# Weights of a linear layer summed over their bits and transposed on TensorE, in the first three tiles of an attention kernel

## What is computed

```
x = x + xattn(layernorm(x), ctx, ctx)                  # x, ctx: 4 x 1024 x 1024 fp32; 16 heads of 64, causal
soft   = sigmoid(pweight) - sigmoid(nweight)           # 1024 x 1024 x 4 bits, fp32
weight = einsum('oin,n->oi', soft, exps * sigmoid(mask_weight)) * scale
bias   = bit_ste(einsum('on,n->o', pbias - nbias, bexps)) * biasscale
x = x + layernorm(x) @ weight.T + bias
```

## Time and profile before

| | |
|---|---|
| median of 3 runs | 1310.44 us (1309.8 to 1312.69) |
| profiled execution | 1313.67 us, its span 1310.7 us |
| busy share of the span | PE 87%, DVE 82%, ACT 71%, POOL 46% |
| granted TensorE clock, mean | 0.944 of 2.4 GHz |
| chain that ended last | PE 62%, DVE 19%, issue 6%, ACT 5%, POOL 3%, DMA 3% |

### The profile page before, as it was taken

One profiled execution on the slowest core, in us unless ns is written; L12 is line 12 of the kernel. 1 busy time (PEld: TensorE's weight loads), 2 busy tenths in 40 slices (PEclk: granted clock), 3 DMA queues, 4 the chain that ended last, 5 costly groups with the idle time before them and its releaser, 6 DMA issues.

```text
span 1310.7 us, 28652 instructions
## 1 busy us (share of the span) xinstructions
PE 1144.8 (87%) x11088; PEld 848.5 (65%) x11088; DVE 1072.6 (82%) x1613; ACT 926.6 (71%) x2011; POOL 599.9 (46%) x717
## 2 busy tenths in 40 slices
PE   1555665589998999999999999999999999999998
PEld 1433444466766677777777677787776677777753
DVE  3588998878897688888898898888988888888861
ACT  1677787567776577777777777777787777777740
POOL 2378666533324574433324954433237744332241
PEclk9867767689999999999999999999999999999999
DMA  6899899243333675433324856434226854320113
GB/s 187 224 223 255 225 267 240 66 106 89 66 81 69 158 168 123 114 81 93 72 82 82 201 121 130 97 82 94 70 64 147 178 116 111 81 66 2 33 41 89
DMA packets 245622, 157.08 MB, mean 120 GB/s; under 512 B 220912, under 2 KB 220912, under 8 KB 245488
## 3 DMA queue, kind: packets, MB, share of 16 engines
q1 hardware_dynamic: 245488, 155.26, 49.5%
HBM read 67.15 MB, written 16.78 MB: 64 GB/s over the span
## 4 chain that ended last, share of the span: by engine, by line
PE 62%; DVE 19%; issue 6%; ACT 5%; POOL 3%; DMA 3%; SPq 1%; ACTq 0%; DVEq 0%; POOLq 0%
PE ffnb L433 20%; PE ptb L401 14%; PE oacc L415 7%; PE slot L388 7%; PE slot L389 7%; DVE pt_lo L570 5%; PE oacc L417 4%; DVE stats L584 3%; DVE mx L563 3%; ACT pt_hi L476 2%; PE slot L433 2%; PE slot L392 2%; DMA qt<-q 1%; DVE y L610 1%; DVE ring L619 1%
## 5 line engine op out<-in xcount | busy, mean ns | idle before, releaser
L570 DVE SCALAR_TENSOR_TENSOR pt_lo<-ptb,pt_hi 128x384 f16<-128x384 f32 (+2 forms) x688 | 382.9, 597 | 117.6 <-ACT pt_hi L476 115.4
L466 ACT ACTIVATE p<-slot,mx 128x512 f32<-128x512 f32 (+7 forms) x512 | 378.0, 747 | 96.1 <-DVE mx L563 94.1
L476 ACT ACTIVATE pt_hi<-ptb 128x384 f16<-128x384 f32 (+2 forms) x688 | 326.4, 527 | 150.2 <-PE ptb L401 149.4
L401 PE MATMUL ptb<-id,p 128*128 128x128 f32 x2304 | 340.8, 289 | 75.9 <-DVE pt_lo L570 75.0
L563 DVE TENSOR_REDUCE mx<-slot 128x1 f32<-128x640 f32 (+7 forms) x352 | 359.5, 1021 | 32.8 <-PE slot L392 30.2
L433 PE MATMUL ffnb<-wt,yt 128*128 128x512 f16 x1440 | 365.3, 381 | 18.6 <-DVE ring L619 15.6
L401 PEld LDWEIGHTS ptb<-id,p 128*128 128x128 f32 x2304 | 259.5, 146 | 87.6 <-issue 84.4
L388 PE MATMUL slot<-kt,qt 128*128 128x128 f16 (+3 forms) x1056 | 278.5, 293 | 38.8 <-DMA qs<-qt 26.5
L753 POOL TENSOR_TENSOR att<-osb 128x256 f32<-128x256 f32 x128 | 98.8, 772 | 398.9 <-ACT osb L483 375.8
L389 PE MATMUL slot<-kt,qs 128*128 128x128 f16 (+3 forms) x1056 | 278.4, 293 | 0.0
L415 PE MATMUL oacc<-v,pt_hi 128*128 128x128 f16 x2304 | 252.3, 224 | 15.3 <-ACT osb L483 13.4
(11 more groups left out here) (64 smaller groups left out, 976.8 us busy)
## 6 DMA issues: line engine op xcount, KB each, us to landing
ring<-in_x_dram SPq DMA_DIRECT2D x32, 512.0 KB, 4.9
cin<-in_ctx_dram SPq DMA_DIRECT2D x32, 512.0 KB, 4.2
qs<-qt SPq DMA_DIRECT2D x64, 256.0 KB, 3.8
out_dram<-ring SPq DMA_DIRECT2D x32, 512.0 KB, 2.9
v<-in_L_ffn_pweight_dram SPq DMA_DIRECT2D x16, 512.0 KB, 4.7
kt<-in_L_ffn_nweight_dram SPq DMA_DIRECT2D x16, 512.0 KB, 5.6
v<-in_L_ffn_nweight_dram SPq DMA_DIRECT2D x8, 512.0 KB, 7.6
kt<-in_L_ffn_pweight_dram SPq DMA_DIRECT2D x8, 512.0 KB, 4.5
```

Of the source, the lines that this page charges most:

```text
L401: last = pe.transpose(ptb[:, c % 2, at * P:(at + 1) * P], p32[:, j.par, k * P:(k + 1) * P], id32[:, :])
L466: last = nc.scalar.activation(p32[:, j.par, hh * j.keys:(hh + 1) * j.keys], slot[:, j.par, base:base + j.keys], ACT.Exp, bias=mx[:, j.par, ...
L476: nc.scalar.activation(pt_hi[:, j.par, P * blocks.start:P * blocks.stop], ptb[:, c % 2, 0:P * len(blocks)], ACT.Copy, scale=P_SCALE).then_ ...
L570: nc.vector.scalar_tensor_tensor(pt_lo[:, j.par, cols], ptb[:, c % 2, 0:P * len(blocks)], P_SCALE, pt_hi[:, j.par, cols], ALU.mult, ALU.su ...
```

## The change

- Chunks are taken in pairs, called units. Unit u goes with job u, for jobs 0 to 15, that is in tiles 0 to 2. There are 6 pairs of buffers.
- The product, the sum over bits and the DMA transpose of the weights are gone. In their place PE does 16 fp32 matmuls a unit: the stationary operand is the difference at one bit (128 weights with a step of 4 elements), the moving operand is the identity times that bit's coefficient, and the four bits add up in the PSUM bank `ffnb`. The result comes out transposed.
- ACT and DVE split it from PSUM straight into `wt` (512 elements a unit).
- `linear_plan` gives each tile from 4 on one linear layer: tile 4 gets one, tile 8 keeps one.
- SP loads x and context of tile 0 first, and the bias is made behind the first scores, in other banks.

```diff
-PAIRS = 4
+UNITS = CHUNKS // 2
+PAIRS = 6
...
 def linear_plan(t):
-    n = steps(t) if t < TILES else 0
-    if t < 5:
+    return [(t - 4, 0, steps(t))] if 4 <= t < TILES else []
...
-        pairs = [(as_f32(v16, 8), as_f32(v16, 9)), (as_f32(v16, 7), as_f32(kt16, 8)),
-                 (as_f32(kt16, 7), as_f32(kt16, 6)), (as_f32(yt, 0), as_f32(yt, 1))]
-        w32 = ring[:, 7, :]
+        pairs = [(as_f32(v16, 9), as_f32(v16, 8)), (as_f32(v16, 7), as_f32(kt16, 8)),
+                 (as_f32(kt16, 7), as_f32(kt16, 6)), (as_f32(v16, 6), as_f32(kt16, 5)),
+                 (ring[:, 7, :], ring[:, 6, :]), (as_f32(v16, 5), as_f32(yt, 0))]
+        coef_diag = as_f32(yt, 1)[:, 0:NBITS * P].rearrange("p (n q) -> p n q", n=NBITS)
         ones32 = y16[:, 0, 0:2, :].bitcast(F32).rearrange("p a b -> p (a b)")
         bits = y16[:, 1, 0, :].bitcast(F32).rearrange("p (a n) -> p a n", a=2)
-        bdiag = norm32[:, :].rearrange("p (j q) -> p j q", j=8)
+        bdiag = bias_row[:, :].rearrange("p (j q) -> p j q", j=8)
         coef = small[:, 14:18]
...
             def load_w(w):
-                reached(sp, w_sum, w - PAIRS + 1)
+                reached(sp, w_turned, (w - PAIRS) // 2 + 1)
                 sp.dma_start(pairs[w % PAIRS][0], pw_t[w // NWCH, w % NWCH]).then_inc(w_in[w % PAIRS], 16)
...
+            load_x(0)
+            load_c(0)
...
+            load_w(0)
             load_x(1)
-            load_w(0)
-            load_x(2)
-            load_w(1)
             turn_k(0)
             load_c(1)
+            load_w(1)
             turn_q(0)
             swap_q(0)
-            load_w(2)
             turn_k(1)
             load_c(2)
             turn_q(1)
+            load_w(2)
             load_w(3)
+            load_x(2)
+            load_w(4)
+            load_w(5)
...
+                    u = FIRST[t] + s + 3
+                    if u < UNITS:
+                        load_w(2 * u)
+                        load_w(2 * u + 1)
...
+            def weights(u):
+                if u == 0:
+                    pe.wait_ge(coef_step, NBITS)
+                    pe.wait_ge(bias_out, 2)
+                reached(pe, w_lo, u)
+                pe.wait_ge(d_ready, 2 * u + 2)
+                for b in range(4):
+                    a = pairs[(2 * u + b // 2) % PAIRS][0].rearrange("p (k n) -> p k n", n=NBITS)
+                    for n in range(NBITS):
+                        last = pe.matmul(ffnb[:, b * P:(b + 1) * P], a[:, b % 2 * P:(b % 2 + 1) * P, n],
+                                         coef_diag[:, n, :], start=n == 0, stop=n == NBITS - 1)
+                last.then_inc(w_turned, 1)
...
             pe.wait_ge(pool_const, 9)
+            scores(JOBS[0])
+            scores(JOBS[1])
             pe.wait_ge(bias_step, 18)
             for j in range(8):
-                last = pe.matmul(slot[:, 0, j * P:(j + 1) * P], ones32[:, :], bdiag[:, j, :], start=True, stop=True)
+                bank = oacc[:, j, :] if j < 4 else ffnb[:, (j - 4) * P:(j - 3) * P]
+                last = pe.matmul(bank, ones32[:, :], bdiag[:, j, :], start=True, stop=True)
             last.then_inc(bias_summed, 1)
...
+                if j.n < UNITS:
+                    weights(j.n)
...
-            def weights_high(o):
-                act.wait_ge(w_sum, NWCH * (o + 1))
-                reached(act, wt_in, 16 * o)
-                nc.scalar.copy(y16[:, 0, :, :], w32.rearrange("p (k c) -> p k c", c=P)).then_inc(w_hi, 1)
+            def weights_high(u):
+                act.wait_ge(w_turned, u + 1)
+                nc.scalar.copy(wt[:, 0, u % 2 * 4:u % 2 * 4 + 4, u // 2 * P:(u // 2 + 1) * P],
+                               ffnb.rearrange("p (k c) -> p k c", c=P)).then_inc(w_hi, 1)
...
+            c_split(0)
             act.wait_ge(small_in, 16 * 7)
             nc.scalar.activation(coef, small[:, 8:12], ACT.Tanh, scale=0.5).then_inc(coef_tanh, 1)
+            q_split(0)
+            chunk_tanh(0)
+            c_split(1)
+            q_split(1)
+            chunk_tanh(1)
+            exponentials(JOBS[0])
+            exponentials(JOBS[1])
             act.wait_ge(bias_summed, 1)
             nc.scalar.copy(bias_row[:, :].rearrange("p (q j) -> p j q", j=8)[:, 0:4, :],
-                           slot[:, 0, 0:512].rearrange("p (j q) -> p j q", j=4)).then_inc(bias_out, 1)
-            c_split(0)
-            q_split(0)
-            c_split(1)
-            q_split(1)
-            exponentials(JOBS[0])
-            exponentials(JOBS[1])
+                           oacc[:, :, :]).then_inc(bias_out, 1)
...
+                if 0 <= j.n - 1 < UNITS:
+                    weights_high(j.n - 1)
                 high_parts(j)
+                if j.n + 1 < UNITS:
+                    chunk_tanh(2 * j.n + 2)
                 if j.n + 2 < len(JOBS):
                     exponentials(JOBS[j.n + 2])
-                w = weight_step(t, s)
-                if w is not None:
-                    weights(w)
+                if j.n + 1 < UNITS:
+                    chunk_tanh(2 * j.n + 3)
...
-            def weights_sum(w):
-                a = pairs[w % PAIRS][0].rearrange("p (k n) -> p k n", n=NBITS)
-                dve.wait_ge(d_ready, w + 1)
-                nc.vector.tensor_tensor(a, a, coef.unsqueeze(1).to_broadcast([P, WCH, NBITS]), ALU.mult
-                                        ).then_inc(w_mul, 1)
-                reached(dve, w_lo, w // NWCH)
-                dve.wait_ge(w_mul, w + 1)
-                nc.vector.tensor_reduce(w32[:, w % NWCH * WCH:(w % NWCH + 1) * WCH], a, AX_X, ALU.add
-                                        ).then_inc(w_sum, 1)
-
-            def weights_low(o):
-                dve.wait_ge(w_hi, o + 1)
-                nc.vector.tensor_tensor(y16[:, 1, :, :], w32.rearrange("p (k c) -> p k c", c=P), y16[:, 0, :, :],
-                                        ALU.subtract).then_inc(w_lo, 1)
-
-            def weights(w):
-                if w >= 5 and w % NWCH == 1:
-                    weights_low((w - 5) // NWCH)
-                if 1 <= w <= CHUNKS:
-                    weights_sum(w - 1)
+            def weights_low(u):
+                dve.wait_ge(w_hi, u + 1)
+                rows, cols = slice(u % 2 * 4, u % 2 * 4 + 4), slice(u // 2 * P, (u // 2 + 1) * P)
+                nc.vector.tensor_tensor(wt[:, 1, rows, cols], ffnb.rearrange("p (k c) -> p k c", c=P),
+                                        wt[:, 0, rows, cols], ALU.subtract).then_inc(w_lo, 1)
...
+            dve.wait_ge(pool_const, 9)
+            for n in range(NBITS):
+                nc.vector.tensor_scalar(coef_diag[:, n, :], id32[:, :], coef[:, n:n + 1], None, ALU.mult
+                                        ).then_inc(coef_step, 1)
+            q_split(0)
...
+                if j.n + 1 < UNITS:
+                    difference(2 * j.n + 2)
                 if j.n > 1 and JOBS[j.n - 2].closes_group:
                     add_attention(JOBS[j.n - 2].group)
+                if j.n + 1 < UNITS:
+                    difference(2 * j.n + 3)
```

More of the change, by code:

```diff
@@ L119 @@
 BIAS = {4: 2, 8: 4, 16: 9}
-Y_LATE = {0: (10, 12, 14), 4: (12, 13, 14), TILES - 3: (12, 13, 14)}
+Y_LATE = {TILES - 3: (12, 13, 14)}
 def q_at(t, s, part):
[L127 to L130, removed]
+    return t + 2 < TILES and s == Q_STEPS[steps(t)][part]
 def y_begun(t, s):
@@ L241, in build @@
         bias_added, ffn_done, res_done = sem("bias_added"), sem("ffn_done"), sem("res_done")
-        th_ready, d_ready, w_mul, w_sum, w_hi, w_lo = (
-            sem("w_" + n) for n in ("tanh", "diff", "mul", "sum", "hi", "lo"))
+        th_ready, d_ready, w_turned, w_hi, w_lo = (sem("w_" + n) for n in ("tanh", "diff", "turned", "hi", "lo"))
         pool_const, coef_tanh, coef_step, bias_step = (
@@ L331, in _ @@
                     if s == 0:
-                        if t >= 6:
-                            for k, _, _ in linear_plan(t - 1)[-1:]:
-                                store(k)
+                        if t >= 5:
+                            store(t - 5)
                         if t + 1 < TILES:
                             swap_q(t + 1)
-                        if t == 8:
-                            turn_y(4)
-                    if s == (0 if 4 < t < 9 else n // 2):
-                        ahead = {5: 7, 6: 8, 7: 9, 8: 10}.get(t, t + 3)
-                        if t != 4 and ahead < TILES:
-                            load_x(ahead)
-                    if t == 8 and s == 3:
-                        store(3)
-                        load_x(11)
-                    w = weight_step(t, s)
-                    if w is not None:
-                        if w >= 1 and w + 3 < CHUNKS:
-                            load_w(w + 3)
-                        if w >= 5 and w % NWCH == 1:
-                            turn_w((w - 5) // NWCH)
+                    if s == n // 2 and t + 3 < TILES:
+                        load_x(t + 3)
                     if s == C_LO[n] and t + 3 < TILES:
@@ L669, in _ @@
```

(27 more changed lines are left out.)

65 lines of the change are left out of this document (17 added, 48 removed).

## The result

| | before | changed |
|---|---|---|
| median | 1310.59 us | 1300.01 us (1298.93 to 1301.84) |
| ratio | 1 | 0.9918 (0.9901 to 0.9935) |
| span of the profiled execution | 1310.7 us | 1298.0 us |
| first maxima of tile 0 / tile 4 / tile 10 | 36.0 / 185.6 / 460.0 us | 31.0 / 229.1 / 446.5 us |
| PE busy, granted clock | 87%, 0.944 | 94%, 0.991 |

The account below looks back on a forecast made before the run. DVE, carrying the weights, was taken to bound the stage before 263 us, PE the rest. 36 + 15 x 9.1 + 22.8 + 218.8 put tile 10 at 414.1, 45.9 us earlier: 1310.4 - 45.9 = 1264.5 us, range 1247 to 1303.

Parts of the forecast that it names:

- transfers that bind: Second rival, jobs with units: DMA transfers bound the period, 11 us a job, 1292 us (10.2 us, 1281); chance 0.20.
- Added on PE: PE's new unit matmuls in the first stage: 16 a unit, 59 to 118 us of PE in all.
- The first rival: Units on PE: strided fp32 loads don't hide, 1427 us, middle 1355; with PE always at 1.2 GHz (1325), chance 0.12.
- P: Period of a job with a unit, tiles 0 to 2: forecast 9.1 us, range 8.4 to 10.1 at chance 0.56.
- end of the first unit: Start of the kernel: unit 0 ends at 36 us, after tile 0's first maxima at about 23.5.
- rest of tile 3 to tile 4: After unit 15: six more jobs of tile 3 at 3.6 us plus 1.2 us of PE, 22.8 us.
- tiles 4 to 9: After the weights: one linear layer each, taking the 218.8 us of tiles 20 to 25.
- chain of tanh and differences: Unit's loop through PE, ACT and POOL at full clock: 17.5 us for two jobs, mean 8.1 us a job.
- the bank loop: At 1.2 GHz, unit j waits for the previous unit's low split from the single bank `ffnb`: 13.2 us a job.
- One job in five at 1.2 GHz: PE's clock in jobs with units: 0.8 x 8.1 + 0.2 x 13.2 = 9.1 us a job.
- the fourth rival: At tile 4: weights ready sooner, but late first y or low PE clock gives it back, no gain; chance 0.02.
- Break-even at P = 12.2: Jobs with units: a period of 12.2 us leaves tile 10 at 460 us, so no gain.

Follow-up runs that it names:

- the first experiment: Changed kernel with each unit matmul reading 128 contiguous elements as stationary operand instead of a step of 16 bytes (sums of other elements): 1270.2 us, ratio 0.9676.
- The bank-first run: Changed kernel with ACT copying the unit out before the attention group and DVE taking the low split before the maxima, same work: 1284.4 us, ratio 0.9784.
- the short units: For 290 to 327 GB/s: changed kernel with ACT's and DVE's unit work put first and one of four bits summed: 1258.4 us, ratio 0.9577.

## Why the prediction was right in its sign and wrong in its size

The direction and the stage were right, and the time lay in the range, which is luck: the upper end, 1303, had been set for transfers that bind, and it was PE that held the period at 10.9 us. The step that failed is the price under "Added on PE": "A unit has 16 matmuls: 7.4 us at 1.2 GHz, 3.7 us at 2.4 GHz". Measured are 7.7 us at either clock. The reading of the bias matmuls as 1.2 GHz ones was sound (a contiguous pass is 0.112 us at full clock and 0.213 at half in the first experiment, and theirs are 0.22 apart). What failed was to carry that price to an operand with a step of 16 bytes. The first rival named this mechanism, priced its far ends and gave it 0.12 on the slower side only, while the middle, a pass of 0.24 us, never entered P.

From the forecast to the measured start of tile 10:

| term | forecast | measured | difference |
|---|---|---|---|
| end of the first unit | 36 us | 43.7 us | +7.7 |
| 15 periods | 9.1 us each | (207.2 - 43.7) / 15 = 10.9 us | +27.0 |
| rest of tile 3 to tile 4 | 22.8 us | 21.9 us | -0.9 |
| tiles 4 to 9 | 218.8 us | 217.4 us | -1.4 |
| tile 10 begins | 414.1 us | 446.5 us | +32.4 |

- *The period.* It is some 7.6 of unit (to the start of the scores behind it), 2.3 of attention and 1.0 of waiting for the bank (12.5 us in 12 jobs). The prediction took its chain of tanh and differences as the period and had the bank loop only for 1.2 GHz. With a long unit PE's own work is longer than the chain, and the bank wait comes on top at full clock too, since the unit's two copies stand behind the attention's. The bank-first run shows this 1.0 us.
- *The clock.* One job in five at 1.2 GHz was assumed, at a price of 5.1 us each (13.2 against 8.1). Between the first and the last unit PE was granted 0.94, which is 12% of the time at half clock, so the share was not far off. The price was wrong for this kernel: a strided pass costs the same at both levels.
- *The start.* x and q came about as forecast (q at 13.4 us for 12.5). The way of q to the first maxima was put at 10.6 to 11 us and took 17.6, behind transfers that share SP's queue. The first unit ended 7.7 us late, and 4 of the 7.7 us are the longer first unit.
- *Rivals.* The transfers didn't bind (ACT waited for no load), and the 232 GB/s that priced this rival were no ceiling: the short units ran at 290 to 327. That its P of 11.0 is near the measured 10.9 is chance. The weights were ready sooner and nothing after tile 4 gave it back, so the fourth rival fell. Break-even at P = 12.2 stands: 10.9 lies 1.26 us under it, which is 18.9 us in 15 periods. Less the 7.7 of the first unit and with the 2.3 of the last two rows of the table that is the 13.5 us by which tile 10 begins earlier (460.0 to 446.5).

With the unit at the assumed length (two bits) the same sum was right to 2 us, but two errors cancel in it. The first unit ended at 39.8 us, 3.8 late, and 15 periods of 8.9 us are 2.8 us short of the forecast ones. The passes of these units don't get longer at half clock, so the 8.9 us also suggest that the 8.1 for the chain at full clock were too low. No run shows that chain by itself. The error that counted was one price, taken from the nearest row without its access pattern.

## What to carry to other kernels

Before a matmul's price is taken from a row, compare the step of its stationary operand as well as its size and type: fp32 with 16 bytes from weight to weight costs at full clock twice what 8 or 4 bytes cost here, and the engine that writes the operand may be able to store it the right way round, as POOL did for nothing. Put the copies that free a single PSUM bank ahead of all else on their engines, once PE is the bound: that gave 15.8 us at tile 4 with the long unit and 4.6 with the short one. And test the parts of a mixed change apart, against the start that the kernel before really had: here the new start gave half to three quarters of what the whole change brought.

## What the runs showed of the hardware

- Loading 128 columns of an fp32 stationary operand took 192 ns contiguous, 196 ns at a step of 8 bytes, and 329 ns at 16 bytes, all at full clock, with passes 0.112, 0.118 and 0.233 us apart. At half clock the contiguous pass was 0.213 us and the strided one still 0.233. With 64 moving columns the strided pass was 0.233 us as well.
- With those 64 columns the granted clock was 0.63 in 100 to 160 us though PE was marked busy 95% of it; with 128 columns it was 0.94 there. The low level cost nothing in the strided passes and 60% in the scores (0.53 against 0.33 us for 384 columns).
- POOL's fp32 difference with a scattered output (step 1 KB inside a row) took 2.37 to 2.57 us by buffer, contiguous 2.35 to 2.60.
- DVE's product of 1024 fp32 elements took 1.33 us in the kernel before and 1.59 to 2.14 us by buffer when two of them and two of POOL's differences fell to each job.
- Issuing the DMA transposes of k and q of tile 0 took SP 5.8 and 5.5 us at 8 and 15 us, with bulk loads in flight, and 1.8 and 2.9 us at 21 and 25 us in the kernel before.
